# One masked pass for the diagonal blocks of a ranking, with new engine orders, in a linear-attention and token-routing kernel

## What is computed

```python
h = layernorm(x)
q = elu(h @ Wq + bq) + 1; k = elu(h @ Wk + bk) + 1      # 16 heads of 8
k = k / sqrt(sum(k*k, -1) + 1e-6); v = h @ Wv + bv
attn = (q @ k.T) @ v                                     # no softmax: q @ (k.T @ v)
x1 = x + layernorm(h + attn @ Wo + bo) * gamma + beta
g = layernorm(x1)
scores = g @ w_router                                    # one number per token
top_idx = top_k(scores, 768)                             # of 1024, per sequence
ffn = g with rows top_idx replaced by gelu(g[top_idx] @ w_block)
return x1 + ffn
```

## Time and profile before

| | us |
|---|---|
| median of 3 runs (lowest to highest) | 113.17 (112.95 to 113.35) |
| the profiled execution, its own time | 112.07 |
| its span in the profile | 110.4 |
| DVE busy | 97.0 (88% of the span), 294 instructions |
| PE busy | 86.9 (79%), 887 instructions |
| ACT busy | 64.2 (58%) |
| POOL busy | 62.1 (56%) |
| comparisons, L716 | 18.8 in 48 instructions |
| tie pass, L727 | 9.0 in 32 instructions |
| mean granted TensorE clock | 0.943 |

### The profile page before, as it was taken

How to read it: one execution, slowest core, us unless ns; L and a number is a source line. 1 busy time by engine, 2 the same in 40 slices (tenths; PEclk the granted TensorE clock), 3 DMA queues, 4 the chain that set the end, 5 groups by cost and what they waited for, 6 DMA issues and landing times.

```text
span 110.4 us, 2594 instructions
## 1 busy us (share of the span) xinstructions
PE 86.9 (79%) x887; PEld 78.8 (71%) x890; DVE 97.0 (88%) x294; ACT 64.2 (58%) x149; POOL 62.1 (56%) x118
## 2 busy tenths in 40 slices
PE   0006999999999999999999999799699997454300
PEld 0004959797399799999999999699599795454200
DVE  5669999692889999989999999989998999999930
ACT  4005489999975873058508998969239979003000
POOL 6791789699900004078798789999289883000000
PEclk9999999999999999999999999999967999998555
DMA  2999000000000000000000000000000000000996
GB/s 68 313 296 252 0 3 3 0 6 0 0 3 0 0 6 0 0 0 0 6 0 0 3 0 6 0 0 0 0 6 0 0 9 3 0 0 6 277 286 198
DMA packets 9637, 4.83 MB, mean 44 GB/s; under 512 B 524, under 2 KB 9624, under 8 KB 9624
## 3 DMA queue, kind: packets, MB, share of 16 engines
q1 hardware_dynamic: 8928, 4.33, 14.7%
q10 hardware_dynamic: 696, 0.33, 1.0%
HBM read 2.56 MB, written 2.10 MB: 42 GB/s over the span
## 4 chain that ended last, share of the span: by engine, by line
PE 40%; DVE 24%; POOL 18%; issue 7%; DMA 3%; ACT 2%; DVEq 1%
PE bank L974 12%; POOL r L288 7%; PE bank L959 6%; DVE beats L716 6%; DVE xb_sb L680 4%; PE bank L951 4%; DVE ties L727 3%; POOL x_sb L303 3%; PE bank L990 3%; PE bank L971 3%; DMA x_sb<-in_L_attn_x_dram 3%; DVE x_sb L752 3%; PE bank L1028 3%; PE bank L1010 2%; PE bank L1009 2%
## 5 line engine op out<-in xcount | busy, mean ns | idle before, releaser
L716 DVE TENSOR_SCALAR beats<-s_row,s_col 128x512 bf16<-128x512 f32 (+3 forms) x48 | 18.8, 450 | 0.2 <-ACT s_row L444 0.2
L974 PEld LDWEIGHTS bank<-wkv_sb,hT 128*128 128x128 f32 x128 | 17.3, 196 | 0.8
L974 PE MATMUL bank<-wkv_sb,hT 128*128 128x128 f32 x128 | 17.2, 278 | 0.0
L437 ACT ACTIVATE norm_sb<-xb_sb,shift,gain 128x128 f32<-128x128 f32 x32 | 13.2, 490 | 5.2 <-POOL shift L298 5.2
L951 PE MATMUL bank<-ident,norm_sb 128*128 128x128 f32 x32 | 5.6, 312 | 9.4 <-ACT norm_sb L371 9.2
L1010 PE MATMUL bank<-ident,hT 128*128 128x128 f32 x64 | 12.4, 275 | 0.0
L1009 PE MATMUL bank<-M_sb,qT 128*128 128x128 f32 x64 | 12.4, 275 | 0.0
L951 PEld LDWEIGHTS bank<-ident,norm_sb 128*128 128x128 f32 x32 | 4.3, 160 | 10.5 <-issue 9.9
L1048 PE MATMUL bank<-ident,beats 128*128 128x128 bf16 x144 | 9.2, 219 | 2.4 <-DVE beats L716 2.4
L430 ACT ACTIVATE x_sb<-bank,r 128x128 f32<-128x128 f32 x32 | 9.3, 367 | 2.9 <-DVE s_col L695 2.9
L1009 PEld LDWEIGHTS bank<-M_sb,qT 128*128 128x128 f32 x64 | 10.3, 192 | 0.3
(11 more groups left out here) (105 smaller groups left out, 236.0 us busy)
## 6 DMA issues: line engine op xcount, KB each, us to landing
out_dram<-x_sb SPq DMA_DIRECT2D x8, 256.0 KB, 3.4
x_sb<-in_L_attn_x_dram SPq DMA_DIRECT2D x7, 256.0 KB, 4.6
x_sb<-in_L_attn_x_dram ACTq DMA_DIRECT2D x1, 256.0 KB, 3.7
wkv_sb<-in_L_attn_Wk_dram SPq DMA_DIRECT2D x1, 64.0 KB, 3.5
wq_sb<-in_L_attn_Wq_dram ACTq DMA_DIRECT2D x1, 64.0 KB, 3.8
wkv_sb<-in_L_attn_Wv_dram SPq DMA_DIRECT2D x1, 64.0 KB, 3.6
wo_sb<-in_L_attn_Wo_dram SPq DMA_DIRECT2D x1, 64.0 KB, 5.0
beta_sb<-in_L_attn_beta_dram SPq DMA_DIRECT2D x1, 64.0 KB, 4.1
```

What stands on the lines that cost most here:

```text
L437: last = nc.scalar.activation(norm_sb[:, t], xb_sb[:, t], ACT.Identity, bias=shift3[:, t:t + 1], scale=gain3[:, t:t + 1])
L716: ins = nc.vector.tensor_scalar(beats[:, b % 2, J, c0:c1], s_row[:, b, c0:c1], s_J, None, ALU.is_le)
L974: last = nc.tensor.matmul(o[:, t * P:(t + 1) * P], hT[:, u, t * P:(t + 1) * P], wkv_sb[:, vector * P:(vector + 1) * P], start=False, stop= ...
```

## The change

The diagonal blocks are no longer compared twice. `compare` starts one tile further right (`P * (J + 1)`), so `compare(b, 3, 0)` and `compare(b, 7, 1)` are gone. `compare_own` takes the place of `tied`: it writes `(s_row <= s_col) * later` into the diagonal block of `beats` itself, where `later` is the mask that `lower` was (column after row), and so settles ties in the same instruction. `row_sums` now waits for both kinds of comparison. `rank` loses the matmul on `ties`, takes the diagonal block of `beats` as one more of its sum, and gets a matmul on a constant (`earlier16`, built on POOL) for the tokens of its own tile; `later_tiles` counts one tile fewer. Unused code for another way of counting (ACCUM, le_count) is taken out, with one small memset. Unit 0 is normalised by DVE alone (NORM1). Function `emptied` has another name. BANK_USES and the lists of PE, DVE, ACT and POOL are all written in another order; SP's is not.

```diff
-    NORM1 = 'HDDADADA'
+    NORM1 = 'DDDADADA'
...
-                    nc.gpsimd.memset(later_tiles[:, J:J + 1], float(T - J))
+                    nc.gpsimd.memset(later_tiles[:, J:J + 1], float(T - 1 - J))
...
-                link(nc.gpsimd.memset(lower[:], 1.0))
-                nc.gpsimd.affine_select(out=lower[:], in_=lower[:], compare_op=ALU.is_gt, fill=0.0, base=0,
+                nc.gpsimd.memset(later[:], 1.0)
+                link(nc.gpsimd.memset(earlier16[:], 1.0))
+                nc.gpsimd.affine_select(out=later[:], in_=later[:], compare_op=ALU.is_gt, fill=0.0, base=0,
                                         pattern=[[1, P]], channel_multiplier=-1)
+                nc.gpsimd.affine_select(out=earlier16[:], in_=earlier16[:], compare_op=ALU.is_gt, fill=0.0, base=0,
+                                        pattern=[[-1, P]], channel_multiplier=1)
...
-                nc.vector.memset(le_count[:], 0.0)
...
-                c0, c1 = (P * J, HW) if part == 0 else (max(P * J, HW), T * P)
+                c0, c1 = (P * (J + 1), HW) if part == 0 else (max(P * (J + 1), HW), T * P)
...
-                if part == 1 and J in (TH - 1, T - 1):
+                if part == 1 and J in (TH - 1, T - 2):
                     ins.then_inc(beats_done, 1)
...
-                    last = nc.vector.scalar_tensor_tensor(out=ties[:, b % 2, I], in0=s_row[:, b, I * P:(I + 1) * P],
-                                                          scalar=s_col[:, T * b + I:T * b + I + 1], in1=lower[:],
-                                                          op0=ALU.is_equal, op1=ALU.mult)
-                last.then_inc(ties_done, 1)
+                    last = nc.vector.scalar_tensor_tensor(out=beats[:, b % 2, I, I * P:(I + 1) * P],
+                                                          in0=s_row[:, b, I * P:(I + 1) * P],
+                                                          scalar=s_col[:, T * b + I:T * b + I + 1], in1=later[:],
+                                                          op0=ALU.is_le, op1=ALU.mult)
+                last.then_inc(own_done, 1)
...
                 pe.wait_ge(beats_done, 2 * b + half + 1)
-                o = take(("sums", SUMS.index((b, half))))
+                pe.wait_ge(own_done, 2 * b + half + 1)
+                o = take(("sums", 2 * b + half))
...
                     nc.tensor.matmul(o[:, i:i + 1], ones16[:], later_tiles[:, i:i + 1], start=True, stop=False)
-                    for J in range(i):
+                    nc.tensor.matmul(o[:, i:i + 1], earlier16[:], ones16[:, 0:1], start=False, stop=False)
+                    for J in range(i + 1):
                         nc.tensor.matmul(o[:, i:i + 1], beats[:, b % 2, J, i * P:(i + 1) * P], ones16[:, 0:1],
                                          start=False, stop=False)
-                    last = nc.tensor.matmul(o[:, i:i + 1], ties[:, b % 2, i], ones16[:, 0:1], start=False, stop=b in ACCUM)
```

More of the change, by code:

```diff
@@ L188, in preln_linear_attention_mod_ffn @@
         DVE_TO = {"D": TH, "H": TH // 2}
-        SUMS = [(b, half) for b in range(B) if b not in ACCUM for half in range(2)]
         block = ctx.enter_context(nc.Block())
@@ L323, in _ @@
             add_beta(5)
+            shifts1(4)
             add_beta(6)
@@ L798, in _ @@
+            key_sums(4)
+            normalise1(6)
+            key_norms(1)
+            mask_vk(0)
+            scale_v(2)
+            scale_v(3)
+            q_half(4)
+            key_sums(5)
+            q_half(5)
+            key_norms(2)
+            scale_v(4)
+            scale_v(5)
+            k_half(6)
+            k_half(7)
+            key_sums(6)
+            key_sums(7)
+            q_half(6)
+            key_norms(3)
             q_half(7)
-            key_sums(5)
-            key_sums(6)
@@ L898, in _ @@
             compare(2, 5, 1)
+            score_cols(7, 0)
+            compare(2, 6, 1)
+            compare_own(2, 0)
+            score_cols(7, 1)
+            compare_own(2, 1)
+            drop(0)
             drop(1)
-            compare(2, 6, 1)
-            compare(2, 7, 1)
             compare(3, 0, 0)
             compare(3, 1, 0)
+            compare_own(3, 0)
             compare(3, 2, 0)
-            compare(3, 3, 0)
             compare(3, 0, 1)
@@ L912, in _ @@
             compare(3, 6, 1)
-            compare(3, 7, 1)
-            tied(2, 0)
-            tied(2, 1)
-            tied(3, 0)
-            tied(3, 1)
+            drop(2)
+            compare_own(3, 1)
             merge(0)
@@ L920, in _ @@
             merge(2)
-            drop(2)
             merge(3)
```

438 lines of the change are left out of this document (196 added, 242 removed).

## The result

| | before | changed |
|---|---|---|
| median of 4 runs, us | 113.06 (111.99 to 113.35) | **114.86** (114.61 to 115.88) |
| ratio, 95% interval | | 1.0178 (1.0131 to 1.0224) |
| the profiled execution, its span, us | 112.07, 110.4 | 115.88, 114.1 |
| first merge starts, us | 100.47 | 104.25 |
| from there to the end of the span | 9.9 | 9.9 |

The change makes the kernel 1.8% slower; 1.3% faster was forecast. The profiled execution of before is 1.0 us faster than its median, that of after 1.0 us slower than its. The two traces therefore lie 3.8 us apart, of which 1.8 stand in the medians.

The account below looks back on a forecast made before the run. With DVE and PE nearly full, the span was first merge start plus 9.9 us, the merge standing behind DVE's comparisons. -3.2 + 1.06 + 0.75 + 0.08, with PE's 0.2, made -1.5: 113.17 to 111.7 us, range 109.3 to 113.6.

Parts of the forecast that it names:

- Term 1: DVE's comparisons ahead of the first merge: narrower blocks and fewer instructions, -3.2 us.
- rival (d): DVE's comparisons do not get cheaper by width, only the eight dropped instructions count; 113.3 us, chance 0.11 together with (b).
- Term 2: DVE's 32 masked comparisons of diagonal blocks cost the same as the old tie pass: 0.
- The tail: The end is the output transfer on full DMA engines: the span ends 9.9 us after the first merge starts.
- Term 7: Ranks on PE, 8 more matmuls each, 0.22 us, covered by other work and the output transfer: 0.
- Term 6: DVE comparisons colliding with POOL's wide adds: two meetings as now, about 0.95 us each, so 0.
- rival (c): Slower: POOL's four adds in a row block comparisons; two more meetings give 113.6 us, three 114.5; chance 0.15.
- Terms 3 and 4: Start with unit 0 normalised on DVE alone, 0; first y half later on PE, y statistics at 46.9, +1.1 us.
- Term 5: DVE's waits behind the first y statistics: +1.85 us new, 1.1 old ones gone, net +0.75 us.
- Rivals (a) and (b): (a) whole gain arrives, 109.1 us, half of that 110, chance 0.22; (b) rank(2) late, 113.1, 0.11 with (d).

Follow-up runs that it names:

- own_old_orders: The comparison part of the change (masks, widths, compare_own, rank) in the kernel before, with that kernel's engine orders almost unchanged; 110.28 us, ratio 0.9786.
- experiment 1: The run of own_old_orders: the comparison part alone, put into the kernel before; 110.28 us, ratio 0.9786.
- small_adds: The changed kernel with POOL's eight gelu_sum adds cut to four columns of one tile; 112.73 us, ratio 0.9984.
- experiment 4: gelu_sum cut to four columns, in the changed kernel (112.73 us) and in the kernel before with only the comparison part of the change (108.8 us).
- changed_no_adds: The changed kernel with all POOL's wide adds, gelu_sum and add_beta, cut to four columns; 110.47 us profiled, 113.17, 113.19 and 113.23 in the others.
- sums11_early: The changed kernel with ACT's copy_sums(1,1) moved ahead of norm_sum(6); 114.33 us, ratio 1.0131 to the kernel before.
- experiment 2: The run of sums11_early: copy_sums(1,1) ahead of norm_sum(6) on ACT in the changed kernel; 114.33 us, ratio 1.0131.
- own_warm: The kernel before with the comparison part of the change, plus 28 extra identity transposes on PE from about 2 us on; 111.12 us, ratio 0.9833.
- after_warm: The changed kernel with 24 extra identity transposes on PE from about 2 us on; 114.84 us, ratio 1.0207.

## Why the prediction was wrong

**What held.** *Term 1:* 2.9 us less work in own_old_orders (92.9 to 90.0 in the ledger), and 2.4 us by the ratio of experiment 1; 3.2 was forecast. The undisturbed durations (small_adds: 283, 349, 417, 479 ns) step by the forecast 65 ns per 128 columns, and rival (d) is out. *Term 2:* 9.0 us for 32 masked comparisons, as the tie pass. *The tail:* 9.9 us from first merge to end in every kernel, from 96.35 (span 106.3) to 118.38 (span 128.3). *Term 7:* drop(3) waits 0.6 us in after and 1.13 in own_old_orders, behind the transfer.

In the terms of the ledger, the forecast was -2.7 us of work, +1.3 of waiting and 0 of held-up time; the traces have -2.3, +3.4 and +2.6.

**Term 6 failed ("collisions: 0, as many as now").** The over-long time rose by 2.6 us, 1.2 of it behind the first y statistics and 1.4 ahead of them. In the late part, the adds began 5 us later than in my walk, because everything ahead was late (2.7 at the first y statistics) and POOL's own operations were slowed (the two from 76.43 took 4.05 us for 1.24); then they fell on comparisons, as rival (c) has it (two meetings more give 113.6, three 114.5). Besides that I left out a whole class: add_beta moved forward on POOL, and I did not look at what it meets. POOL's timeline, then DVE's, in after:

```profile
18.22 1.27 POOL L271 TENSOR_TENSOR xb_sb<-x_sb,beta_sb 128x512 f32<-128x512 f32 x1
...
28.67 2.51 POOL L271 TENSOR_TENSOR xb_sb<-x_sb,beta_sb 128x512 f32<-128x512 f32 x2
...
17.76 2.08 DVE L605 TENSOR_SCALAR norm_sb<-x_sb,bn,r 128x128 f32<-128x128 f32 x4
...
30.00 1.33 DVE L635 TENSOR_TENSOR k_tmp<-k_seed 128x128 f32<-128x128 f32 x1
```

The four instructions of a normalisation take 2.08 instead of 1.11 and key_norms' first step 1.33 instead of 0.28. The trace of before had such a meeting too, which the prediction's "two in this trace" passed over (POOL's timeline, then DVE's, in before):

```profile
22.05 1.28 POOL L272 TENSOR_TENSOR xb_sb<-x_sb,beta_sb 128x512 f32<-128x512 f32 x1
...
22.53 1.67 DVE L608 TENSOR_SCALAR norm_sb<-x_sb,bn,r 128x128 f32<-128x128 f32 x4
```

In the medians, the gelu_sum adds cost the new orders only 0.6 us more than the old (2.1 and 1.5, experiment 4). The section of the Trainium skill named in Term 6 ("SBUF — State Buffer", "Who interferes with whom") says that a VectorE instruction with two SBUF inputs contends with a GpSimd instruction that reads SBUF. The trace agrees: key_norms' first step (+1.04) and the masked comparisons (3.19 for 1.13) have two such inputs, and POOL's adds read SBUF. In the prediction I had applied it to wide comparisons only.

**Terms 3 and 4 failed by size.** The first y statistics came at 49.56; 46.9 was forecast. Three profiles divide the 2.7 us, by differences between single executions. DVE's timeline, in changed_no_adds:

```profile
47.50 0.76 DVE L660 BATCH_NORM_STATS2 bn<-bank 128x6 f32<-128x256 f32 x2 [0.35 <-PE bank L986]
```

and in after:

```profile
49.56 0.76 DVE L661 BATCH_NORM_STATS2 bn<-bank 128x6 f32<-128x256 f32 x2 [0.36 <-PE bank L987]
```

Without adds and with the short start it is 47.5: the walk was 0.6 too early. sums11_early has the adds and the short start: 48.48, so the meetings with add_beta cost 1.0. After has the long start: 1.1 more. The prediction has no term for the pace of the first projections. They go at the lower clock: in after, k_proj(0) from 10.11 and v_proj(0) from 13.05 to 15.07, in before only until 12.37. "PE's steady work begins about where it did" was wrong for these two executions: PE began sooner and then kept to the lower pace for 2.7 us longer. But the same list also ran with the slow stretch ending at 12.83, so this part is one of chance between executions. How much of it is in the median, and what sets the end of that pace, stays open.

**Term 5 failed by one wait.** Behind the first y statistics DVE is idle for 3.4 us where 1.85 was forecast; in before it was 1.35, with gaps that the earlier trace rows doesn't list, for 1.1. The y half waits came out smaller (0.43 for 0.65, and one of 0.31 for two of 0.4), and drop(2) waits 0.74 for 0.4, since PE's 36 row-sum matmuls take 3.80 us from 96.95, with a granted clock of 0.62 in 96 to 100. But drop(1), at 1.96, is in no term. I walked the chain for rank(2) and never rank(1)'s, in which ACT's list puts norm_sum(6), and with it POOL's late roots, ahead of copy_sums(1,1). The chain is shown in the trace. Its worth is small: moving that copy gave 0.5 us, inside the intervals (experiment 2), since other waits and meetings took its place.

**So,** by the ratios: the comparison is worth -2.1% (2.4 us), the orders cost +3.9% (4.4 us). Of these, gelu_sum's adds explain 0.6 us and the place of copy_sums(1,1) 0.5, neither clear of noise. What the start costs wasn't isolated, and no single edit that keeps the whole computation recovered more than 0.6 us. So that the new orders make the loss is shown; which of their moves makes it is argued from single profiles and in the main stays open. The rest is shown only as a sum: DVE's idle time is 2.6 us higher in after than in own_old_orders. Rivals (a) and (b) are out. (c) named one of the two mechanisms, meetings, with too small a list of what can be met; the larger part in the trace is waiting.

## What to carry over

Try a cheaper operation in the order that exists before adopting a new order with it: here the one was worth 2.1% and the other took back nearly twice that. When POOL work over SBUF moves, list every DVE operation beside its new place, with all two-input and wide ones, and allow for POOL being late; four adds in a row need all of DVE's work beside them to be harmless. For each wait of the engine that sets the end, walk its whole chain through all engines, not just the chain whose place the change moved.

## What the runs showed of the hardware

- DVE's and POOL's SBUF operations hold each other up in both directions. DVE is held by up to about 1.1 us per meeting with a 128x512 add of 1.27 us (0.96 to 1.06 in most); POOL's four-column operation took 2.40 us at 76.43 beside a row of DVE's operations, against 0.20 undisturbed.
- Making the adds a quarter as long does not reduce this in sum. Late comparisons were held for 0.1 to 0.26 us each, and one instruction of 0.28 us was held through a whole row of short adds, to 1.76 us.
- PE's first matmuls run at the lower level of its clock, eight in 1.92 us, not 1.05. The clock row reads 1.00 there (after, 5 to 12 us) only because the trace has no clock record before the pace changes; durations of rows of one form show it. The end of that stretch moved between 12.83 and 16.11 us for the same list.
- Warming matmuls can bring the full pace forward and still gain nothing: in own_warm the first projections took 1.05 us from 11.16 on, at an idle time of 2.37 us behind the warming, and the median was 111.12 us against 110.28. In after_warm the granted clock fell to 0.50 again.
- The kernel without wide adds took 110.47 us once and 113.2 three times on one chip. One execution's profile alone can mislead by that much.
